# A fourth slot for the input bands, and neighbour sums ahead of the lower halves of differences on VectorE

## The reference

```python
g = group_norm(x)                       # 32 groups, no scale or shift
res = conv3x3(g, W_id, b_id)            # all 8 images, 64 -> 64 channels
# from image 0 alone, one map for all images:
cA, cH, cV, cD = swt2_level3(g[0])      # wavelet filters along rows and columns
low  = attention(cA, ...)               # 1x1 convolutions, a pooled scale per channel
high = attention(stack(cH, cV, cD), ...)
out = leaky_relu(conv3x3(concat(low, high), W_enc, b_enc), 0.01)
return x + out + res                    # out is added to every image
```

## Time and profile before

| | |
|---|---|
| time, median of 3 runs | 1819.07 us (1810.22 to 1823.49) |
| profiled execution, its time | 1814.87 us |
| profiled execution, its span | 1813.1 us |
| busy share of the span: TensorE, VectorE, ScalarE, GpSimd | 97%, 80%, 68%, 30% |
| granted TensorE clock, mean | 0.994 |
| DMA, mean over the span | 216 GB/s |

### The profile page before, as it was taken

How to read it: one execution, slowest core, us unless ns; L and a number is a source line. 1 busy time by engine, 2 the same in 40 slices (tenths; PEclk the granted TensorE clock), 3 DMA queues, 4 the chain that set the end, 5 groups by cost and what they waited for, 6 DMA issues and landing times. The chain is left out here.

```text
span 1813.1 us, 69228 instructions
## 1 busy us (share of the span) xinstructions
PE 1761.4 (97%) x31540; PEld 1470.2 (81%) x31540; DVE 1450.2 (80%) x1926; ACT 1238.6 (68%) x1339; POOL 545.5 (30%) x365
## 2 busy tenths in 40 slices
PE   9999999999999999989999999999999999999997
PEld 9997999999999999965577797767966756967676
DVE  5665578778777887668989889888889888888886
ACT  5555666666666666667776777767776767766774
POOL 0005788888888888640000000000000000000000
PEclk9999999999999999999999999999999999999999
DMA  8884399888888888458998998998989989989994
GB/s 186 245 296 126 122 274 227 212 219 216 212 215 215 215 215 206 100 125 204 235 234 223 239 239 226 240 240 229 238 224 236 247 213 232 242 219 230 249 234 140
DMA packets 132964, 391.84 MB, mean 216 GB/s; under 512 B 49884, under 2 KB 50656, under 8 KB 118464
## 3 DMA queue, kind: packets, MB, share of 16 engines
q1 hardware_dynamic: 132672, 387.43, 82.7%
HBM read 258.88 MB, written 128.45 MB: 214 GB/s over the span
## 5 line engine op out<-in xcount | busy, mean ns | idle before, releaser
L1766 PE MATMUL ps<-big,tail 64*64 64x448 f16 x3840 | 323.3, 353 | 11.8 <-DVE ps L1961 7.8
L1766 PE MATMUL ps<-pool_of 64*64 64x448 f16 x5184 | 302.5, 352 | 7.9 <-DVE pool_of L1625 4.2
L1766 PE MATMUL ps<-pool_of,tail 64*64 64x448 f16 x4896 | 300.1, 349 | 0.7 <-issue 0.7
L1766 PE MATMUL ps<-big,pool_of 64*64 64x448 f16 x3552 | 278.5, 352 | 17.1 <-DVE ps L1961 11.9
L1292 DVE BATCH_NORM_STATS2 pool_of<-big 128x6 f32<-128x448 f32 x392 | 232.2, 616 | 76.4 <-DMA big<-in_x 76.3
L1766 PEld LDWEIGHTS ps<-pool_of 64*64 64x64 f16 x5184 | 196.2, 107 | 68.0 <-issue 10.1
L1766 PEld LDWEIGHTS ps<-pool_of,tail 64*64 64x64 f16 x4896 | 189.6, 106 | 59.3 <-issue 1.3
L1066 PE MATMUL ps<-pool_of 112*128 112x246 f16 x1344 | 218.8, 271 | 1.7 <-DVE pool_of L1280 0.8
L1070 PE MATMUL ps<-pool_of 112*128 112x168 f16 x1344 | 217.8, 243 | 0.0
L1766 PEld LDWEIGHTS ps<-big,tail 64*64 64x64 f16 x3840 | 169.0, 107 | 57.9 <-DVE ps L1961 10.4
L1069 PE MATMUL ps<-pool_of 112*128 112x90 f16 x1344 | 201.3, 206 | 0.0
(11 more groups left out here) (252 smaller groups left out, 3809.8 us busy)
## 6 DMA issues: line engine op xcount, KB each, us to landing
out<-tail SPq DMA_DIRECT2D x448, 224.0 KB, 3.6
big<-in_x SPq DMA_DIRECT2D x392, 224.0 KB, 5.2
pool_of<-in_x SPq DMA_DIRECT2D x139, 560.0 KB, 7.4
tail<-in_x SPq DMA_DIRECT2D x69, 560.0 KB, 7.4
pool_of<-row_filtered SPq DMA_DIRECT2D x110, 224.0 KB, 4.0
row_filtered<-big SPq DMA_DIRECT2D x2, 6272.0 KB, 22.8
pool_of<-in_x SPq DMA_DIRECT2D x30, 392.0 KB, 7.1
row_filtered<-big SPq DMA_DIRECT2D x4, 1568.0 KB, 9.2
```

Of the source, the lines that this page charges most:

```text
L1766: mm = pe.matmul(psum[bank + r][C * k:C * k + C, 0:NT], wt[i % 2][lanes, h, s, kx, :], v[u][lanes, rows_of(k), kx:kx + W], start=False, st ...
```

## The change

A fourth slot `xs[3]` is placed where `base` and `twice` lay. `base` is split into two halves: the loaded half goes to the memory of the statistics, the derived half is first made in the fourth slot and then copied by GpSimd (`keep`) into `tail`, where the buffer `made` lay; weights are built through the memory of the sums instead of `made`. `twice` moves into the odd half of `stage[1]`; `double` waits for the stores of the minimal band before. On VectorE `build_part` and `neighbour_sums(q+1)` go ahead of `diffs_low(q)`. The load of band 3 waits for the copy, the first weights and the end of the map.

```diff
-XS = 3
+XS = 4
 # encoder, end of its SyncE program
             ahead.load(sp, 2)
+            ahead.first_kept(sp)
+            sp.wait_ge(map_done, NE)
+            ahead.load(sp, 3)
 # encoder, end of its GpSimd program
             both_rows(NE - 1)
+            pool.wait_ge(conv_done, 2 * NE)
+            ahead.keep(pool)
 # main
-        xs = [pooled(0, RH * W), pooled(RH * W, RH * W), carve(RH * W)]
-        base = pooled(2 * RH * W, SET_N).rearrange("p (s k e) -> p s k e", s=NSET, k=3)
-        twice = pooled(2 * RH * W + SET_N, 4 * W).rearrange("p (r n) -> p r n", r=2)
+        xs = [pooled(0, RH * W), pooled(RH * W, RH * W), carve(RH * W), pooled(2 * RH * W, RH * W)]
+        base = [v.rearrange("p (s k e) -> p s k e", s=NSET // 2, k=3) for v in (early[:, V_N + HI_N:V_N + HI_N + TMP_N], carve(TMP_N))]
+        early_base = xs[3][:, 0:TMP_N].rearrange("p (s k e) -> p s k e", s=NSET // 2, k=3)
+        twice = stage[1][:, :, :, W:NT]
+        def keep(pool):
+            pool.tensor_copy(base[1].rearrange("p s k e -> p (s k e)"), early_base.rearrange("p s k e -> p (s k e)")).then_inc(kept, 1)
+        def first_kept(sp):
+            sp.wait_ge(kept, 1)
+            sp.wait_ge(building, 11)
 # sync
-            load(sp, 3)
-            load(sp, 4)
+            load(sp, XS)
+            load(sp, XS + 1)
             for q in range(NW):
                 store_direct(q)
                 if q:
                     store_minimal(q - 1)
-                load(sp, 2 * q + 5)
-                load(sp, 2 * q + 6)
+                load(sp, 2 * q + XS + 2)
+                load(sp, 2 * q + XS + 3)
 # double, on ScalarE
                 act.wait_ge(m2_done, j + 1)
                 if j:
                     act.wait_ge(b_seeded, j)
-                act.activation(twice, a_bank, ACT.Identity, scale=-2.0, bias=lane(mean_r2, i)).then_inc(twice_ready, 1)
+                    act.wait_ge(stored[1], 64 * j)
+                act.activation(twice, a_bank.rearrange("p r (g w) -> p r g w", g=2), ACT.Identity, scale=-2.0, bias=lane(mean_r2, i)).then_inc(twice_ready, 1)
 # neighbour_sums, on VectorE
+                if j:
+                    dve.wait_ge(sums_split, j)
                 landed(dve, k)
 # odd_rows, on VectorE
                 dve.wait_ge(odd_done, j + 1)
-                if j:
-                    dve.wait_ge(stored[1], 64 * j)
+                dve.wait_ge(b_seeded, j + 1)
 # order on VectorE
                 if q > 0:
                     odd_rows(q - 1)
-                if q >= 0:
-                    diffs_low(q)
-                if q + 1 < NW:
-                    neighbour_sums(q + 1)
                 i, b = direct(q + 1) if q + 1 < ND else (B, 0)
                 if i + 1 < B and b in DIRECT[2:4]:
+                    dve.wait_ge(sums_split, q + 1)
                     build_part(dve, i + 1, DIRECT.index(b) - 2)
+                if q + 1 < NW:
+                    neighbour_sums(q + 1)
+                if q >= 0:
+                    diffs_low(q)
                 if q + 1 < ND:
                     read_direct(q + 1, 0)
```

More of the change, by code:

```diff
@@ L81 @@
 Link = namedtuple("Link", "cleared einv_ready b32_in act_rows dve_rows first_split emx emax_part emax_all spread_max sx stat_in unit")
-Ahead = namedtuple("Ahead", "load weights_load dummies pads norms spread build normed high full split edges root partners sets spread_rows clear first_seed conv_first conv_rest")
+Ahead = namedtuple("Ahead", "load weights_load dummies pads norms spread build normed high full split edges root partners sets keep first_kept spread_rows clear first_seed conv_first conv_rest")
 def input_transform():
@@ L1450, in main @@
     with ExitStack() as s5:
[L1451 removed]
+        tail = sb(s5, "tail", [P, RH * W + 4 * NT * 2 + V_N + SET_N + SET_N // 2])
         late = [0]
@@ L1471, in main @@
         assert AT_S + 2 * CH * W <= SMALL_AT - NREC * 6
[L1472 to L1475 removed]
+        xs = [pooled(0, RH * W), pooled(RH * W, RH * W), carve(RH * W), pooled(2 * RH * W, RH * W)]
+        assert 3 * RH * W <= D_EVEN_AT
         x_hi = [f16_rows(pooled(AT_HI0, HI_N), RH), f16_rows(pooled(AT_HI0 + 2 * HI_N, HI_N), RH)]
[L1477 removed]
+        x_lo = [f16_rows(pooled(AT_HI0 + HI_N, HI_N), RH), f16_rows(early[:, V_N:V_N + HI_N], RH)]
         sums = pooled(AT_S, 2 * CH * W)
[L1479 removed]
+        made = sums[:, 0:TMP_N].rearrange("p (s k e) -> p s k e", s=NSET // 2, k=3)
         lanes_of = pooled(SMALL_AT - NREC * 6, C + 10 * B)
@@ L1482, in main @@
         inv, m_out, r_out, v_one, v_half, v_neg, neg_two, mean, mean_r, mean_r2 = [lanes_of[:, C + B * k:C + B * k + B] for k in range(10)]
-        diag = early[0:C, RH * W:RH * W + B * C].rearrange("p (i e) -> p i e", i=B)
+        diag = early[0:C, V_N:V_N + B * C].rearrange("p (i e) -> p i e", i=B)
         r_rows = pooled(AT_R, B * C).rearrange("p (i e) -> p i e", i=B)
@@ L1543, in main @@
         building = sem(top, "building")
-        built = sem(top, "built")
+        kept = sem(top, "kept")
         TOP, BOTTOM = 0, NB - 1
@@ L1732, in build_part @@
                 dve.wait_ge(sets_made, 6)
+            if i == 1 and h == 1:
+                dve.wait_ge(kept, 1)
             dve.wait_ge(building, n)
-            dve.tensor_tensor(flat, base[:, 3 * h:3 * h + 3, :, :].rearrange("p s k e -> p (s k) e"),
+            dve.tensor_tensor(flat, (base[h] if i or h == 0 else early_base).rearrange("p s k e -> p (s k) e"),
                               r_rows[:, i, :].unsqueeze(1).broadcast_to((P, 9, C)), ALU.mult).then_inc(building, 1)
@@ L1960, in seed_odd @@
                     dve.wait_ge(odd_read, 2 * j)
-                dve.tensor_tensor(b_bank, a_bank, twice, ALU.add).then_inc(b_seeded, 1)
+                dve.tensor_tensor(b_bank.rearrange("p r (g w) -> p r g w", g=2), a_bank.rearrange("p r (g w) -> p r g w", g=2), twice, ALU.add).then_inc(b_seeded, 1)
             def odd_rows(j):
@@ L1975, in vector @@
                     odd_rows(q - 1)
+                i, b = direct(q + 1) if q + 1 < ND else (B, 0)
+                if i + 1 < B and b in DIRECT[2:4]:
+                    dve.wait_ge(sums_split, q + 1)
+                    build_part(dve, i + 1, DIRECT.index(b) - 2)
+                if q + 1 < NW:
+                    neighbour_sums(q + 1)
                 if q >= 0:
                     diffs_low(q)
-                if q + 1 < NW:
-                    neighbour_sums(q + 1)
-                i, b = direct(q + 1) if q + 1 < ND else (B, 0)
-                if i + 1 < B and b in DIRECT[2:4]:
-                    build_part(dve, i + 1, DIRECT.index(b) - 2)
                 if q + 1 < ND:
@@ L2032, in main @@
                       normed=lambda act: act.wait_ge(normed, 1), high=high, full=full, split=split, edges=edges, root=root_of, partners=partners,
-                      sets=sets, spread_rows=spread_rows, clear=clear, first_seed=first_seed, conv_first=conv_first, conv_rest=conv_rest)
+                      sets=sets, keep=keep, first_kept=first_kept, spread_rows=spread_rows, clear=clear, first_seed=first_seed, conv_first=conv_first, conv_rest=conv_rest)
         return Programs(sync, tensor, scalar, vector, gpsimd), ahead
```

7 lines of the change are left out of this document (3 added, 4 removed).

## The result

The changed kernel takes 2039.43 us (median of 4 runs, 2033.67 to 2047.71) against 1817.56 us for the kernel before in the same comparison: ratio 1.1226, 95% interval 1.1169 to 1.1284, so 12% slower. Its profiled execution took 2040.02 us with a span of 2038.2 us, 225.1 more than before. In the rows of the changed kernel `double` is line 1895, `full` 1617, `split` 1624, `seed_odd` 1979, both reads of a direct band 1972, `neighbour_sums` 1946, `diffs_low` 1964, `diffs_high` 1878, `high` 1611, the stores 1848, the loads 1589, the matmuls 1781.

A forecast was written before the change was run, and what follows sets the result against it. TensorE was busy 97% of the span; the change makes a ring through the stores the bound: 54 loops of 20.76 us (+159.4), end +5.3, start +3, +167.7 on 1813.1, about 1982 us; range 1930 to 2050.

The forecast's parts named there:

- The edit that decides: `twice` moves into `stage[1]`: `double` must wait for the previous minimal band's four stores, pushed back by 3.6 us.
- The ring: Stores, `double`, `full`, `split`, VectorE's work up to `read_direct(1)`, next stores: 20.76 us a loop against 17.13; chance 0.86 for 19.86 to 22.06.
- fixed parts: Parts of the loop besides the stores' landing: `double` to `split` 3.24 us, `split` to the next r 8.48 us.
- all three terms of the sum: 54 longer loops +159.4 us, the last loop +5.3, the start +3; together +167.7 on the span.
- The order on VectorE: Neighbour sums fill the wait before `diffs_low`: nothing in a plain loop; 15 us of TensorE's stalls saved, bounds 0 and 19.7.
- The landing: Last minimal store lands 3.7 us after issue, at r + 9.01; loads spread over longer time speak for less.
- r: End of `read_direct(q+1, 1)` on VectorE in each loop of the image stage; it releases the next direct stores.
- the estimate of 2.5 us for a store: From the skill's page, 2.0 us fixed plus bytes over 436 GB/s for 224 KB: ring 19.5 us, time about 1915.
- The start: GpSimd's copy of derived sets, 1.4 us, delays the loads of bands 3 and 4: 3 us taken, bounds 0 and 4.
- The end: In the last loop `double(55)` starts at r + 8.5, without loads, rather than r + 3.28: +5.3 us.
- Rival 3, TensorE's clock: TensorE idles 3.6 us a loop; a clock low for 12 us would make it the bound, 2106 us; chance 0.05.
- TensorE's wait for `seed_odd`: Build loops cost nothing extra any more, so the 19.7 us of stalls vanish into the longer loop.

The follow-up runs named there:

- the order alone: Kernel before with build and neighbour sums ahead of the lower halves of differences, three slots, `twice` in its own buffer: 1809.52 us, ratio 0.9965.
- the last mended kernel: Changed kernel with own buffer for `twice`, band 4 loaded ahead and band 5 loaded behind the first direct stores: 1799.12 us, ratio 0.9891.
- the mended kernels: Changed kernel with own buffer for `twice` and band 4 loaded ahead, 1800.38 us; the same with band 5 behind the first direct stores, 1799.12 us.
- the run with minimal stores only: Changed kernel without the direct bands' stores and the waits for them, so half of the output is missing: 1897.52 us, ratio 1.0437.
- the kernels with two copies: Changed kernel with own buffer for `twice`, derived sets kept in two gaps so `keep` is two copies: 1806.53 us; later kernels build on it.
- the run with two stores for a band: Changed kernel with two stores of 448 KB for a band rather than four of 224 KB: 2062.86 us, ratio 1.1346.
- the one with late loads: Changed kernel, but SyncE issues a loop's two loads only when `double` has run: 2034.41 us, ratio 1.1194.
- the mended one: Changed kernel with own buffer for `twice` and band 4 ahead, 1800.38 us; with two stores for a band there, 1811.78 us.

## Why the prediction was right, and where its sizes were off

**The edit that decides** was named: the wait of `double`, and the kernel before with that wait alone takes 2031 us. The ring was named step by step, and its fixed parts measured 3.25 (forecast 3.24) and 8.54 us (8.48). The measured time lies 11 us under the upper end of the range: all three terms of the sum, taken up below, missed on the same side, and the range held because it allowed for landings of up to 5.0 us.

**The order on VectorE**: in a plain loop it shortens nothing, as said; without the wait it takes the 19.7 us of stalls to 1.8 (the order alone) and 1.6 (the last mended kernel). The forecast gain of 15 us, had the wait been free, is what the mended kernels show: 18.

**The landing** is the term that was mis-sized: r + 9.04 was forecast for `double`, r + 9.87 was measured, 0.83 x 54 = 45 us. The failed step is in the sum: one loop's last store, 3.7 us after its issue, stood for 54 loops, and the guess beside it was that thinner loads would make it less. Followed over the 54 loops of each trace, the step comes apart. In the changed kernel the eighth store is issued at r + 5.32 in the mean, as forecast (r + 5.31), lands 4.45 us after its issue, not 3.7, and `double` starts 0.11 us after the landing, not 0.03: 0.75 and 0.08 us. And the change did not make the landing longer. In the kernel before, the same store took 4.42 us in the mean of its 54 loops, 3.59 to 6.01; the loop that was read has the third quickest of the 54. With 4.42 and 0.11 the forecast's own sum gives a ring of 21.6 us and a time of about 2026. The median over all 448 stores (3.6 us) hides this, because the first seven of the eight took 3.3 to 3.8 us in the mean. One sum beside it is rounded: the estimate of 2.5 us for a store gives a ring of 19.6 us and about 1919, not 19.5 and 1915; nothing hangs on it.

Why the last of a burst takes longest is less clear. The last loop of the changed kernel in which all eight stores are issued, with no load left, shows it at its largest. Each row is one issue: the first, fourth, seventh and eighth store (the DMA view's columns are count, size and us to landing).

```profile
out<-tail SPq DMA_DIRECT2D x1, 224.0 KB, 2.8
...
out<-tail SPq DMA_DIRECT2D x1, 224.0 KB, 3.3
...
out<-tail SPq DMA_DIRECT2D x1, 224.0 KB, 4.1
...
out<-tail SPq DMA_DIRECT2D x1, 224.0 KB, 5.4
```

The last was issued at 1996.70 and `double` began when it had landed:

```profile
1996.70 0.84 SPq L1848 DMA_DIRECT2D out<-tail  x1
```

```profile
2002.25 1.01 ACT L1895 ACTIVATE tail<-ps,pool_of 128x896 f32<-128x896 f32 x1 [7.32 <-DMA out<-tail]
```

The windows of the stretch (length, busy us by engine, granted clock, DMA share, GB/s):

```profile
1993.00:1995.00 2.00, 2.00 (x52) 1.20 (x44) 2.00 (x3) 1.93 (x2) 0.00 (x0) 1.00 1.00 229
1995.00:2000.00 5.00, 5.00 (x112) 2.98 (x104) 3.34 (x3) 0.00 (x0) 0.00 (x0) 1.00 0.85 271
2000.00:2002.20 2.20, 0.25 (x8) 0.00 (x0) 0.00 (x0) 0.00 (x0) 0.00 (x0) 1.00 0.05 16
```

SyncE issues 224 KB every 0.6 to 0.7 us, some 330 to 380 GB/s, and 229 to 271 are moved, so up to 2000 us a store that is issued later queues longer. The 2.2 us from there to the landing of the eighth are no queue of bytes: the engines are nearly idle (the last section comes back to them). So two things lengthen the landing in this loop, and how they share the mean of 4.45 us is not shown. The runs do not single out one cause. Holding the loads back left the landing as it was (4.40 us), so it is not the loads. Halving the number of DMAs only moved the time from the issues to the landing, which speaks for the bytes; yet leaving out four of the eight took 0.4 us off the landing and no more, and even then the last of four took 4.02 us where the one ahead of it took 3.26. Why the last store takes the longest stays open. What is shown is its price: in each of the twelve kernels profiled here the last store of the burst has the longest mean landing, and it is the one that a ring of this kind waits for.

**The start**: 3 us forecast, 10.9 measured. The copy on GpSimd took 2.55 us, not 1.4, and not because of its 576 columns: in the run with minimal stores only the same copy took 0.66 us. Both times it began within 0.02 us of VectorE's `differences`. In the changed kernel the copy is longer by about the other's 2.0 us; in the other run `differences` is longer, 2.52 us rather than 2.01, by about the length of the copy. In the kernels with two copies the one of 192 columns took 2.1 to 2.2 us there and the one of 384 behind it 0.50. So the two engines seem to take turns, and the copy's time depends on which goes first. First the changed kernel, then the run with minimal stores only:

```profile
810.85 2.55 POOL L1733 COPY tail<-pool_of 128x576 f32<-128x576 f32 x1
810.87 2.01 DVE L1953 TENSOR_TENSOR tail<-tail 128x1792 f32<-128x1792 f32 x1
```

```profile
811.84 0.66 POOL L1733 COPY tail<-pool_of 128x576 f32<-128x576 f32 x1
811.86 2.52 DVE L1952 TENSOR_TENSOR tail<-tail 128x1792 f32<-128x1792 f32 x1
```

The larger miss was the landing again: three bands are issued at once, and the six DMAs land a median of 10.8 us after issue, where 7.4 was taken for one at a time; band 4 came 10.7 us late for the neighbour sums.

```profile
pool_of<-in_x SPq DMA_DIRECT2D x6, 560.0 KB, 10.8
```

**The end**: 5.3 forecast, 7.2 measured. Of the 1.9 us, 0.4 are the landing (`double` at r + 8.93 rather than r + 8.5). The other 1.6 lie between `double` and `seed_odd`, 4.65 us rather than 3.02, and they are the price of TensorE's clock: the last loop has no further band to work on, so `seed_odd` waits for `m1`, and after a gap of 5.50 us the granted clock is 0.50 from 2022 to 2026. From the start of `m1` to `seed_odd` it takes 3.59 us, against 1.96 at a clock of 1.00 before.

```profile
2023.01 0.96 PE L1781 MATMUL ps<-big,tail 64*64 64x448 f16 x8 [5.50 <-ACT tail L1895]
...
2026.60 1.10 DVE L1979 TENSOR_TENSOR ps<-ps,tail 128x896 f32<-128x896 f32 x1 [7.30 <-PE ps L1781]
```

```profile
2022.00:2026.00 4.00, 2.99 (x33) 1.48 (x36) 0.00 (x0) 0.96 (x1) 0.00 (x0) 0.50 0.00 0
```

The three terms together: 48 (45 for the landing, 3 for `split` to r), 8 and 2 us more than forecast, 225.1 against 167.7.

**Rival 3, TensorE's clock**, was right in its rows and did not come true as a bound. Around a gap of the changed kernel (windows as above, the loop shown before):

```profile
1913.00:1917.00 4.00, 0.00 (x0) 0.00 (x0) 0.00 (x0) 0.97 (x2) 0.00 (x0) 1.00 0.97 268
1917.00:1920.00 3.00, 2.91 (x32) 1.54 (x36) 0.72 (x1) 3.00 (x3) 0.00 (x0) 0.52 0.73 167
1920.00:1924.00 4.00, 4.00 (x84) 2.44 (x80) 4.00 (x3) 1.96 (x2) 0.00 (x0) 0.93 0.27 60
```

After 4 us without a matmul the granted clock is 0.52 for 3 us, its lower level of 1.2 GHz, then 1 again. That costs some 1.5 us (an estimate: half of the 3 us), inside the reserve of over 4 us that TensorE has in such a loop (21.64 less the forecast's 17.1); the mean clock over the span is 0.964, against 0.994. The Trainium skill ("TensorE: Matmul & The Clock Gate", Why this matters for your kernels) says that an idle gap between bursts of matmuls can bring the lower clock back, and this gap agrees. In the loops it bears nothing on the time, since TensorE is not in the ring; in the last one it costs the 1.6 us above.

**TensorE's wait for `seed_odd`** was said to vanish; 26 waits remain, 20.7 us in all. By rows of the forecast's own trace `seed_odd` ends some 6.8 us after `double` starts (3.24, then 2.50 for `split` and 1.09 for `seed_odd`), and TensorE is through with `m1` and the direct rows 6.1 after (1.0 for `double` and 5.1), so a wait of well under a microsecond was to be expected in each loop; it is no loss, since TensorE would otherwise wait for `double`.

## What to carry to other kernels

A buffer that is shared with the source of a store inherits the landing of the last of its stores as a wait; before it is moved there, follow the waiting instruction to the next issue of those stores, and if the way leads back to it, add up the ring, because it, not the busiest engine, sets the loop. Take the landing from the last store of a burst and as a mean over many loops, not from the median over all stores. A reordering that fills a wait needs its data earlier: here the order gains 8 us alone and 18 together with the slot that feeds it, and the slot was paid for with a tile that sat on the path.

## What the runs showed of the hardware that was not expected

A store of 448 KB is issued in as short a time as one of 224 KB: the median of the issues is 0.62 us in the run with two stores for a band and 0.60 in the one with late loads. Yet the longest take 2.9 and 1.8 us, and a burst of four takes 5.0 us in the mean, one of eight 6.0. SyncE is held up within the burst; by what, no run shows. The rows give the shortest, median and longest issue in ns, then first and last start and count; the first is the run with two stores for a band.

```profile
L1847 SPq DMA_DIRECT2D out<-tail x224: 528/615/2887, 818.9 to 2057.5; - x112
```

```profile
L1848 SPq DMA_DIRECT2D out<-tail x448: 466/599/1780, 818.9 to 2034.4; - x150
```

Fewer, larger DMAs were slower here both times, by 23 us in the changed kernel and by 11 in the mended one.

In the last loop shown above, the bytes of the eight stores were nearly all moved by 2000 us, yet the last landed at about 2002.2: in the 2.2 us between, the share of the 16 DMA engines was 0.05, less than one of them at work. It looks as if the semaphore had waited for one late engine of the 16; no run was made to show it, and this store's 5.4 us are the longest of that kernel's eighth stores in the 54 loops.
